# Edge products of the first chunk, moved into the input's normalisation, in a four-layer graph network on one core

## The reference

```python
h = jnp.maximum(_layernorm(x, axis=-1), 0.0)
...
hW = h @ W
hp = (node_adj > 0).astype(hW.dtype) @ hW
hm = (node_adj < 0).astype(hW.dtype) @ hW
e_plus = jax.nn.leaky_relu(jnp.concatenate([hp, hm], axis=1) @ a, ALPHA)[:, 0]
e_minus = jax.nn.leaky_relu(jnp.concatenate([hm, hp], axis=1) @ a, ALPHA)[:, 0]
```

## Time and profile before

| | |
|---|---|
| runs, median of 3 | 2944.71 us (2942.32 to 2945.97) |
| the profiled execution | 2943.5 us, of which its span is 2941.7 us |
| busy in the span | PE 2200.8 us (75%), DVE 2026.0 (69%), ACT 1501.7 (51%), POOL 99.4 (3%) |
| DMA | 638.37 MB, mean 217 GB/s |
| chain that ended last, by engine | PE 60%, DVE 16%, issue 14%, ACT 4%, SP's queue 3%, DMA 3% |

### The profile page before, as it was taken

One profiled execution on the slowest core, in us unless ns is written; L12 is line 12 of the kernel. 1 busy time (PEld: TensorE's weight loads), 2 busy tenths in 40 slices (PEclk: granted clock), 3 DMA queues, 4 the chain that ended last, 5 costly groups with the idle time before them and its releaser, 6 DMA issues.

```text
span 2941.7 us, 20195 instructions
## 1 busy us (share of the span) xinstructions
PE 2200.8 (75%) x5939; PEld 952.6 (32%) x5939; DVE 2026.0 (69%) x2428; ACT 1501.7 (51%) x1447; POOL 99.4 (3%) x152
## 2 busy tenths in 40 slices
PE   4665444444789999999988399920089995999998
PEld 3222111111334444444433244410033332444443
DVE  7986899888679888889956644569799995000000
ACT  1005888888767777777736523310088883100000
POOL 1001100100100000000000000000000000000000
PEclk9757777776899999999998699965599997999999
DMA  7999888887633223233130088737766662989895
GB/s 259 387 389 336 302 319 328 322 312 289 251 127 101 100 100 129 100 104 109 60 143 0 1 287 278 256 119 226 273 217 229 214 228 98 304 299 305 299 312 168
DMA packets 176772, 638.37 MB, mean 217 GB/s; under 512 B 11776, under 2 KB 16176, under 8 KB 133296
## 3 DMA queue, kind: packets, MB, share of 16 engines
q1 hardware_dynamic: 161408, 572.86, 56.5%
q0 software_dynamic: 15280, 64.47, 5.5%
HBM read 597.24 MB, written 40.04 MB: 217 GB/s over the span
## 4 chain that ended last, share of the span: by engine, by line
PE 60%; DVE 16%; issue 14%; ACT 4%; SPq 3%; DMA 3%; DVEq 1%; POOL 0%; ACTq 0%; POOLq 0%
PE bank L584 22%; PE bank L749 15%; PE bank L709 8%; DVE arena L1342 8%; PE bank L657 8%; SPq L264 2%; PE bank L714 2%; DVE arena L1321 1%; DVE arena L1205 1%; PE bank L572 1%; DMA arena<-in_adj 1%; PE bank L604 1%; DVE arena L1130 1%; PE bank L549 1%; PE bank L605 1%
## 5 line engine op out<-in xcount | busy, mean ns | idle before, releaser
L584 PE MATMUL bank<-arena 128*128 128x512 f32 x1536 | 661.6, 594 | 13.3 <-DVE arena L1427 13.3
L549 PE MATMUL bank<-arena 128*128 128x512 f32 x512 | 258.7, 668 | 294.2 <-ACT arena L851 233.7
L749 PE MATMUL bank<-arena 128*128 128x512 f32 x1024 | 443.4, 594 | 29.6 <-ACT arena L1082 29.6
L1342 DVE CUSTOM_DVE_ANT_0 arena<-arena 128x2048 f32<-128x2048 bf16 x192 | 435.5, 2317 | 28.0 <-ACT arena L844 17.2
L1427 DVE TENSOR_TENSOR arena<-arena 128x2048 f32<-128x2048 f32 x192 | 433.2, 2282 | 4.0 <-ACT arena L888 2.1
L844 ACT ACTIVATE arena<-arena,nmx 128x2048 f32<-128x2048 f32 x192 | 384.5, 2002 | 72.8 <-DVE nmx L1342 58.6
L584 PEld LDWEIGHTS bank<-arena 128*128 128x128 f32 x1536 | 292.6, 191 | 382.1 <-issue 381.9
L888 ACT ACTIVATE arena<-arena 128x2048 f32<-128x2048 f32 x128 | 244.5, 1911 | 142.7 <-DVE arena L1416 142.7
L1659 DVE TENSOR_TENSOR arena<-arena,bank 128x512 f32<-128x512 f32 x8 | 5.3, 686 | 416.3 <-PE bank L731 416.3
L749 PEld LDWEIGHTS bank<-arena 128*128 128x128 f32 x1024 | 194.2, 191 | 269.6 <-issue 239.7
L709 PE MATMUL bank<-arena 128*128 128x512 f32 x512 | 238.9, 610 | 24.8 <-DVE arena L1627 24.8
(11 more groups left out here) (232 smaller groups left out, 2093.2 us busy)
## 6 DMA issues: line engine op xcount, KB each, us to landing
arena<-in_adjT SPq DMA_DIRECT2D x384, 1024.0 KB, 5.2
arena<-in_adj SPq DMA_DIRECT2D x128, 1024.0 KB, 5.1
mask_d<-arena POOLq DMA_DIRECT2D x64, 512.0 KB, 7.0
arena<-mask_d SPq DMA_DIRECT2D x64, 512.0 KB, 3.7
arena<-e_d POOLq DMA_DIRECT2D x6, 1024.0 KB, 11.7
arena<-nm_d POOLq DMA_DIRECT2D x6, 1024.0 KB, 7.0
arena<-gat_d POOLq DMA_DIRECT2D x6, 1024.0 KB, 6.7
arena<-in_x SPq DMA_DIRECT2D x4, 512.0 KB, 6.8
```

Of the source, the lines that this page charges most:

```text
L549: last = pe.matmul(banks[2][:], H[:, t, :], groups[4 + g % 4][:, b, :], start=(t == 0), stop=(t == T - 1))
L584: last = pe.matmul(banks[B * half + b][:], hW[:, t, h * C:(h + 1) * C], probs[k % 4][:, b * CH:(b + 1) * CH], start=(t == 0 and h == 0), s ...
L749: last = pe.matmul(banks[B * half + b][:], stationary[:, t, :], ring[slot][:, b * CH:(b + 1) * CH], start=(t == 0), stop=(t == T - 1))
L1342: v.tensor_tensor_reduce(logits[k % 3], mask, e_row, FAR_UNIT, FAR, ALU.add, ALU.min, nmx[:, k:k + 1]).then_inc(S["logits_ready"], 1)
```

## The change

The masks and products of chunk 0 no longer wait for the whole input. The pieces of work are put into the input loop of each engine:

- DVE clears V19 and `sums` ahead of everything. For input group q from 2 on, it makes the masks of edge group q - 2 between the statistics and the normalisation of group q, and splits the values of group q - 2 behind the normalisation (`edge_masks`, `split_values`). The last two groups follow the loop. The split is the same five operations, on the 24 values of four tiles instead of the 192 of all; there are eight such splits.
- ACT copies the values group by group (`copy_values`), and they alternate between banks 5 and 6; `edge_values` waits for the copy of two groups before.
- TensorE does the products of edge group k - 3 behind the transposes of group k and the values of group k - 1 (`edge_group`); the last three groups follow the loop. It waits for each group's split, not for one split of all.
- For chunk 0 the masks of groups 0 and 1 wait for no products, as nothing has used the buffers yet. Chunks 1 to 7, and what follows, stay as they were. SP's and POOL's programs are unchanged.

```diff
--- before.py
+++ after.py
@@ -498,18 +498,34 @@
 
             def edge_values(k):
                 pe.wait_ge(S["turn_copied"], k + 1)
+                if k >= 2:
+                    pe.wait_ge(S["v_copied"], k - 1)
                 for t in range(B * k, B * k + B):
-                    last = pe.matmul(banks[5][:, 6 * t:6 * t + 6], HT[:, t * P:(t + 1) * P], U[:], start=True, stop=True)
+                    last = pe.matmul(banks[5 + k % 2][:, 6 * t:6 * t + 6], HT[:, t * P:(t + 1) * P], U[:], start=True, stop=True)
                 last.then_inc(S["v_ready"], 1)
+
+            def edge_group(q, g):
+                plus, minus = banks[(3, 0)[q % 2]], banks[(4, 1)[q % 2]]
+                if q == 0:
+                    pe.wait_ge(S["v19_ready"], g + 1)
+                pe.wait_ge(S["masks_ready"], q * (2 * G) + 2 * (g + 1))
+                for b in range(B):
+                    t = B * g + b
+                    first, end = t == 0, t == T - 1
+                    pe.matmul(plus[0:VC, :], V19[:, t, :], mask_pos[g % 2][:, b, :], start=first, stop=end)
+                    last = pe.matmul(minus[NEG0:NEG0 + VC, :], V19[:, t, :], mask_neg[g % 2][:, b, :],
+                                     start=first, stop=end)
+                last.then_inc(freed[g], 1)
 
             for k in turn(0):
                 if k:
                     edge_values(k - 1)
+                if k >= 3:
+                    edge_group(0, k - 3)
             edge_values(G - 1)
-            pe.wait_ge(S["v19_ready"], 1)
-
 
             pe.wait_ge(S["const_loaded"], 16 * N_LOADS)
+
             def edge_columns(q):
 
                 pe.wait_ge(S["sums_copied"], 2 * q + 2)
@@ -518,16 +534,8 @@
                 last.then_inc(S["edge_cols_summed"], 1)
 
             for q in range(Q):
-                plus, minus = banks[(3, 0)[q % 2]], banks[(4, 1)[q % 2]]
-                for g in range(G):
-                    pe.wait_ge(S["masks_ready"], q * (2 * G) + 2 * (g + 1))
-                    for b in range(B):
-                        t = B * g + b
-                        first, end = t == 0, t == T - 1
-                        pe.matmul(plus[0:VC, :], V19[:, t, :], mask_pos[g % 2][:, b, :], start=first, stop=end)
-                        last = pe.matmul(minus[NEG0:NEG0 + VC, :], V19[:, t, :], mask_neg[g % 2][:, b, :],
-                                         start=first, stop=end)
-                    last.then_inc(freed[g], 1)
+                for g in range(G - 3 if q == 0 else 0, G):
+                    edge_group(q, g)
                     if g == 2 and q:
                         edge_columns(q - 1)
             edge_columns(Q - 1)
@@ -778,6 +786,11 @@
                 act.activation(chunk, banks[0][:], ACT.Copy).then_inc(S["chunk_evacuated"], 1)
                 act.wait_ge(S["chunk_turned"], q + (8 * u + 1))
 
+            def copy_values(k):
+                act.wait_ge(S["v_ready"], k + 1)
+                act.activation(V[:, B * k:B * k + B, :].rearrange("p t v -> p (t v)"),
+                               banks[5 + k % 2][:, 6 * B * k:6 * B * k + 6 * B], ACT.Copy).then_inc(S["v_copied"], 1)
+
             for q in range(Q):
                 root(0, q)
                 if q == 0:
@@ -785,9 +798,11 @@
                     act.activation(U[:], banks[4][:, 0:6], ACT.Copy).then_inc(S["u_ready"], 1)
                 else:
                     turn_copy(0, q - 1)
+                if q >= 2:
+                    copy_values(q - 2)
             turn_copy(0, Q - 1)
-            act.wait_ge(S["v_ready"], G)
-            act.activation(V.rearrange("p t v -> p (t v)"), banks[5][:, 0:6 * T], ACT.Copy).then_inc(S["v_copied"], 1)
+            copy_values(Q - 2)
+            copy_values(Q - 1)
 
 
             act.wait_ge(S["sums_cleared"], 1)
@@ -1171,40 +1186,54 @@
                 v.tensor_scalar(h_of, h_of, 0.0, None, ALU.max).then_inc(S["h_ready"], 1)
                 dve.wait_ge(S["h_ready"], q + (G * l + 1))
 
+            ch(v.memset(V19, 1.0))
+            v.memset(sums, 0.0).then_inc(S["sums_cleared"], 1)
+
+            def split_values(k):
+
+                dve.wait_ge(S["v_copied"], k + 1)
+                tiles = slice(B * k, B * k + B)
+                for part in range(3):
+                    src = V[:, tiles, :] if part == 0 else VR[:, tiles, :]
+                    dst = V19[:, tiles, 1 + 6 * part:7 + 6 * part]
+                    if part < 2:
+                        ch(v.tensor_copy(dst, src))
+                        tt(VR[:, tiles, :], src, dst, ALU.subtract)
+                    else:
+                        v.tensor_copy(dst, src).then_inc(S["v19_ready"], 1)
+
+            def edge_masks(q, g):
+                dve.wait_ge(loaded[g], q * 16 + 16)
+                if q == g:
+                    d = diagonal_blocks(g)
+                    ch(v.tensor_tensor(d, d, not_i[:].unsqueeze(1).broadcast_to([P, B, P]), ALU.mult))
+
+                if g >= 2:
+                    dve.wait_ge(freed[g - 2], q + 2)
+                elif q:
+                    dve.wait_ge(freed[g + 6], q + 1)
+                v.tensor_scalar(mask_pos[g % 2], groups[g], 0.0, None, ALU.is_gt).then_inc(S["masks_ready"], 1)
+                v.tensor_scalar(mask_neg[g % 2], groups[g], 0.0, None, ALU.is_lt)\
+                    .then_inc(S["masks_ready"], 1)
+
             for q in range(Q):
                 if q % 2 == 0:
                     dve.wait_ge(x_loaded[q // 2], 16)
                 variances(0, q)
+                if q == 2:
+                    dve.wait_ge(S["first_loaded"], 64)
+                if q >= 2:
+                    edge_masks(0, q - 2)
                 normalise(0, q, H[:, B * q:B * q + B, :])
-            ch(v.memset(V19, 1.0))
-
-            v.memset(sums, 0.0).then_inc(S["sums_cleared"], 1)
-            dve.wait_ge(S["v_copied"], 1)
-
-            for part in range(3):
-                src = V if part == 0 else VR
-                dst = V19[:, :, 1 + 6 * part:7 + 6 * part]
-                if part < 2:
-                    ch(v.tensor_copy(dst, src))
-                    tt(VR, src, dst, ALU.subtract)
-                else:
-                    v.tensor_copy(dst, src).then_inc(S["v19_ready"], 1)
-
-            dve.wait_ge(S["first_loaded"], 64)
-            for q in range(Q):
+                if q >= 2:
+                    split_values(q - 2)
+            split_values(Q - 2)
+            edge_masks(0, Q - 2)
+            split_values(Q - 1)
+            edge_masks(0, Q - 1)
+            for q in range(1, Q):
                 for g in range(G):
-                    dve.wait_ge(loaded[g], q * 16 + 16)
-                    if q == g:
-                        d = diagonal_blocks(g)
-                        ch(v.tensor_tensor(d, d, not_i[:].unsqueeze(1).broadcast_to([P, B, P]), ALU.mult))
-
-                    if g >= 2:
-                        dve.wait_ge(freed[g - 2], q + 2)
-                    else:
-                        dve.wait_ge(freed[g + 6], q + 1)
-                    v.tensor_scalar(mask_pos[g % 2], groups[g], 0.0, None, ALU.is_gt).then_inc(S["masks_ready"], 1)
-                    v.tensor_scalar(mask_neg[g % 2], groups[g], 0.0, None, ALU.is_lt)\
-                        .then_inc(S["masks_ready"], 1)
+                    edge_masks(q, g)
             dve.wait_ge(S["const_loaded"], 16 * N_LOADS)
 
             dve.wait_ge(freed[G - 1], Q + 1)
```

## The result

The changed kernel takes 2950.31 us (median of 8 runs, 2944.96 to 2953.23), the kernel before 2942.72 beside it (8 runs, 2938.29 to 2945.97). The ratio is 1.0022, with a 95% interval of 1.0012 to 1.0033: **slower by 7.6 us**, where +7.8 was forecast. The profiled execution took 2953.23 us.

The account below looks back on a forecast made before the run. The edge pass was taken as paced by its loads, DVE's pace a second bound. Sixth load +7.2 and start 0.6 gave +7.8: 2943.5 + 7.8 = 2951.3, plus 1.2 to the median, 2952.5 us; range 2944 to 2957.

Parts of the forecast that it names:

- The wait that decides: Chunk 0's masks wait for TensorE to free buffers from two groups earlier: 1.8 us each, groups 4 to 7 taking 9.45 us.
- h(7): End of the normalisation of input group 7, forecast at 72.5 us against about 47.5 before.
- h(1): End of the normalisation of input group 1, taken as 19.77 us.
- The start of the train: Chunk 1's sixth load, heading the unbroken loads, goes out at 80.7 and lands 5.4 later at 86.1: +7.2 us.
- I take 0: Delay from the hT store, moved to about 75 us at the train's start: bounds 0 to 2.7 us, taken as 0.
- The third rival: hT store delays the train 2.7 us and group 0's split takes 2.0, not 1.0: +11.5, near 2956.2 us; chance 0.08.
- DVE's bound: In the edge pass, chunk 0's masks end at 82.9; seven chunks of 20.1 reach 223.7, 5.3 us late; loads are later.
- The 0.6 charged for the start: Time the old train of loads lost in starting, between chunk 1's first and sixth landings, charged again: 0.6 us.
- leave the path behind h(7): The two clears, the larger 3.47 us, move ahead of the first input and no longer delay what follows the input stage.
- The clock: Rival: TensorE rises to 2.4 GHz in each burst, the mask wait vanishes, pass 3.3 us earlier, about 2941.4; chance 0.14.
- the first two: Rivals: TensorE's clock rises in every burst (0.14); or in some, or splits and waits overlap better, 0 to +5 us (0.12).
- The pause: Rival: filling the early DMA pause, loads run unbroken from 39.4 and gain up to 20 us, 2925; chance 0.04.

Follow-up runs that it names:

- the first experiment: Changed kernel with the products of chunk 0 one input group earlier (edge group k-2, not k-3): 2939.44 us against 2941.66 for the kernel before.
- the second experiment: Changed kernel with four pairs of mask buffers in chunk 0 instead of two: 2943.89 us against 2941.66 for the kernel before.
- The third experiment: Changed kernel with hT stored in four pieces, each behind two turned groups: 2948.89 us against 2941.66 for the kernel before.
- The fifth experiment: Kernel before the change with only the two clears moved ahead of the input loop: 2941.54 us against 2941.03.
- the tenth kernel: Changed kernel with splits on GpSimd, products one group earlier, four mask buffers, hT in pieces, small loads early: 2933.99 us against 2942.16 for the kernel before.
- the sixth: As an experiment: kernel before the change with the clears ahead of the input and the first two masks ahead of the split: 2939.46 us against 2941.03.
- the eighth experiment: Changed kernel with products one group earlier, four mask buffers in chunk 0, hT in pieces, splits on GpSimd: 2935.51 us against 2941.03 for the kernel before.

## Why the prediction was right

**The wait that decides** came as stated: before masks of groups 2 to 5, 1.98 us each (1.8 forecast), with input groups 4 to 7 standing 9.45 us apart, the forecast figure. h(7) stands 52.45 us after h(1) (73.03 - 20.58; forecast 72.5 - 19.77 = 52.7). The first and second experiments show that it is the cause of the loss.

**The loads** went out at 39.9, 49.3, 58.8, 68.2 and 77.7, each 0.4 to 0.5 us behind the forecast, less than the 0.8 by which h(1) was late. The DMA queue stood at one wait of 13.7 us and four of 8.9 instead of the five of near 9 that were forecast. From 40 to 60 us the DMA moved 107 GB/s, against 387 in the steady stretch.

**The start of the train** is where the sum was off. The sixth load was issued 60.7 us after h(1) (81.3 - 20.58; forecast 80.7 - 19.77 = 60.9), but landed after 6.9 us, not 5.4. The term "I take 0" for the hT store failed: the store and the fifth load together were to need 8.2 us of about 9, but the fifth landed 10.4 us after the store's issue (77.7 + 7.8 - 75.1), and the sixth 2.7 behind it. The third experiment sizes the term at 1.8 us of the pass. The third rival had this mechanism at 2.7 us; its other half, a split of 2.0 us, did not come: five operations took 36.12 + 0.18 - 35.25 = 1.05 us, as forecast.

**DVE's bound**: those of chunk 1 followed chunk 0's at 83.53 (82.9 forecast, h(1) 0.8 later), and the loads set the end, as DVE's last wait at 225.07 for adjT shows.

**The 0.6 charged for the start** came out as 0.5, but not where it was charged. Counted from chunk 1's first, the fifth to the ninth load land 2.7 us apart (85.5, 88.2, 90.9, 93.6, 96.3), so the start cost nothing. The next one comes 4.2 us later, at 100.5:

```profile
L264 SPq DMA_DIRECT2D arena<-in_adjT x1: 386/386/386, 90.1 to 90.1; - x1
...
DMA to landing us min/median/max: 10.4/10.4/10.4
```

Why it does stays open. That the term nearly fits is luck.

**The end**: 228.16 against 226.2. Of the 2.0 us, 0.8 is the later h(1), and 1.2 remain: 1.5 from the sixth load's landing, less 0.2 in its issue and 0.1 in the train. The passes differ by 9.0 us, the pair of profiles by 9.7 (2953.23 - 2943.5), the medians by 7.6. So the forecast of 7.8 is 1.2 short of the pass that it describes, and that it meets the medians within 0.2 is in part luck: why the medians moved by less than the pass is not shown.

**One sentence was wrong and cost nothing**: that the two clears "leave the path behind h(7)". The fifth experiment shows that they lay beside TensorE's and ACT's last values. No gain was counted for them apart from the whole.

**The rivals.** The clock did not rise: every burst's transposes took 1.12 us, so the first two fell. The store's half of the third came, its split did not. What the first would have brought, a wait that vanishes, the first experiment reached by order alone, with a pass 1.5 us shorter than before (forecast 3.3). The pause was not worth 20 us: the loads did not run without a break from 39.9 on, and even the tenth kernel, in whose input stage DVE waits for no products, gains 8.2.

## What to carry to other kernels

When work is interleaved into a loop, follow the buffer it needs round its whole circle: who frees it, and behind what that engine has queued the freeing work. Here a lag of three groups with two buffers made two engines wait for each other once in each group, and a lag of two gave 2.2 us gained, where the change had lost 7.6. The early start of five transfers was worth nothing here, as the sixth, from which the steady train runs, came later; look for the load behind which the train no longer breaks.

## What the runs showed of the hardware that was not expected

- The start of the kernel is not fixed: not_i ended TensorE's first wait between 15.3 and 17.5 us in the ten profiles with the loads in this order, and h(1) moved with it from 19.7 to 21.9 us. Two profiles are compared from h(1), not from zero.
- The time behind the pass (profiled total less pass end) lay between 2718.4 and 2726.4 us over the twelve profiles, with no relation to the edits that I can see. It is the same work in all of them; why it varies stays open. It is of the size of the effects studied here, so where the trace of the pass and the median differ (most for the change itself, +9.0 and +7.6, then for the second experiment, +0.8 and +2.2, and the sixth, -2.9 and -1.6), the trace says where the time went and the median is the one that counts.
- On GpSimd one of the first two small operations behind a wait took 1.1 us (in the eighth experiment the first in five splits, 1.12 to 1.15, and the second in two, 1.08, behind a first of 0.62 to 0.66), and those that follow 0.21 to 0.29 (128 x 24 values); on DVE all five took 0.18 to 0.19.
- A load of 1 MB that runs alone landed 5.0 to 5.2 us after its issue (the first four of chunk 1 in the changed kernel); in the full train one lands every 2.74 us.
